# Chosen-token experts: one expert of two batches per unit, with the gated rows as weights

## The reference

```python
k = min(max(int(l * C / e), 1), l)                    # l = 748, C = 2, e = 8: k = 187
S = softmax(x @ Wg); G, I = top_k(swapaxes(S, 1, 2), k)   # each expert of each batch chooses 187 steps
ex = take_along_axis(x[:, None], I[..., None], axis=2)
hmid = gelu(einsum('bekh,ehf->bekf', ex, W1) + b1)    # 128 -> 256
out = einsum('bekf,efh->bekh', hmid, W2) + b2         # 256 -> 128
new_x = zeros.at[batch, I].add(G[..., None] * out)    # h = h + new_x
```

## Time and profile before

| what | us |
| --- | --- |
| median of 3 runs | 2656.92 |
| span of the profiled execution | 2655.1 |
| TensorE busy | 2389.5 (90%) |
| VectorE busy | 2026.5 (76%) |
| ScalarE busy | 1665.8 (63%) |
| GpSimd busy | 1124.6 (42%) |
| `chosen_ffn`, first turned tile to last statistics | 1267.9 to 1640.3 |

### The profile page before, as it was taken

One profiled execution on the slowest core, in us unless ns is written; L12 is line 12 of the kernel. 1 busy time (PEld: TensorE's weight loads), 2 busy tenths in 40 slices (PEclk: granted clock), 3 DMA queues, 4 the chain that ended last, 5 costly groups with the idle time before them and its releaser, 6 DMA issues. The chain is left out here.

```text
span 2655.1 us, 52098 instructions
## 1 busy us (share of the span) xinstructions
PE 2389.5 (90%) x16443; PEld 1819.7 (69%) x16443; DVE 2026.5 (76%) x3647; ACT 1665.8 (63%) x3127; POOL 1124.6 (42%) x1338
## 2 busy tenths in 40 slices
PE   7989699999999999854899997999849999999993
PEld 7989455444445444343799997888738887888882
DVE  4555589999999999489688887788776666787775
ACT  3345267777777777743566664555527777777772
POOL 0016002223223222323777773444337774666664
PEclk9999699999999999975899998999969999999997
DMA  3108633333333323054111112400021113777749
GB/s 90 36 12 319 193 56 50 62 62 56 48 62 62 57 47 62 18 152 149 42 38 38 39 38 68 164 0 0 1 81 52 51 52 103 243 240 247 243 143 277
DMA packets 161298, 249.19 MB, mean 94 GB/s; under 512 B 41645, under 2 KB 106902, under 8 KB 154233
## 3 DMA queue, kind: packets, MB, share of 16 engines
q1 hardware_dynamic: 128888, 208.77, 29.1%
q0 software_dynamic: 19712, 38.13, 4.9%
q10 hardware_dynamic: 12544, 0.39, 0.2%
HBM read 155.24 MB, written 93.41 MB: 94 GB/s over the span
## 5 line engine op out<-in xcount | busy, mean ns | idle before, releaser
L1014 ACT ACTIVATE probs<-score 128x748 f32<-128x748 f32 (+1 forms) x768 | 568.4, 794 | 117.2 <-PE score L839 115.8
L943 DVE TENSOR_REDUCE part_max<-to_dve 128x1 f32<-128x512 f32 (+1 forms) x768 | 479.7, 683 | 84.0 <-PE to_dve L820 83.6
L2762 DVE TENSOR_TENSOR m_hid_lo<-m_up,m_hid_hi 128x512 fp32r<-128x512 f32 x408 | 279.9, 687 | 157.1 <-ACT m_hid_hi L2735 157.1
L820 PE MATMUL to_dve<-k_stack,q_stack 48*128 48x512 f32 (+3 forms) x1536 | 351.4, 367 | 20.9 <-DMA k_stack<-k_parts 20.1
L839 PE MATMUL score<-q_stack,k_stack 49*128 49x374 f32 (+1 forms) x1536 | 317.3, 389 | 3.1 <-ACT probs L1014 1.0
L839 PEld LDWEIGHTS score<-q_stack,k_stack 49*128 49x128 f32 (+1 forms) x1536 | 162.0, 181 | 225.0 <-ACT probs L1014 199.7
L876 PE MATMUL o_sum<-probs,v_sb 128*17 128x374 f32 (+1 forms) x3072 | 315.6, 483 | 0.1
L2658 POOL DMA_INDIRECT e_sums<-m_gated,m_row_in x216 | 212.6, 984 | 162.3 <-DVE m_gated L2780 109.2
L820 PEld LDWEIGHTS to_dve<-k_stack,q_stack 48*128 48x128 f32 (+1 forms) x1536 | 223.1, 187 | 79.7 <-DVE part_max L943 36.6
L740 POOL TENSOR_TENSOR o_rows<-o_raw,inverse 128x384 f32<-128x384 f32 x32 | 26.9, 842 | 589.7 <-DVE inverse L953 589.7
L1371 POOL DMA_INDIRECT f_row_in_c<-c_rows,c_ids x192 | 218.4, 1137 | 75.2 <-issue 49.6
(11 more groups left out here) (411 smaller groups left out, 6003.8 us busy)
## 6 DMA issues: line engine op xcount, KB each, us to landing
m_weights<-e_records SPq DMA_DIRECT2D x54, 1028.0 KB, 6.9
q_stack<-q_parts SPq DMA_DIRECT2D x192, 93.5 KB, 3.1
k_stack<-k_parts SPq DMA_DIRECT2D x192, 93.5 KB, 4.2
e_slots<-blank SPq DMA_DIRECT2D x54, 260.0 KB, 3.9
m_row_in<-e_slots SPq DMA_DIRECT2D x54, 260.0 KB, 3.3
m_weights<-e_sums SPq DMA_DIRECT2D x16, 640.0 KB
e_records<-l_parts SPq DMA_DIRECT2D x16, 512.0 KB, 3.7
v_rows<-v_out SPq DMA_DIRECT2D x16, 408.0 KB, 5.9
```

The lines of the kernel that those rows point to most:

```text
L820: last = pe.matmul(ring[i % RING][0:ROWS[c], at_col:at_col + keys.stop - keys.start], q_stack[its_slot][rows, j, c * P:c * P + ROWS[c]], k ...
L943: dve.tensor_reduce(part_max[0:ROWS[c], k, j, c, 0:1], ring[i % RING][0:ROWS[c], :], AX.X, ALU.max).then_inc(used, 1)
L1014: act.activation(probs[0:n, s % 2, m, 2 * j:2 * j + 2, :], score[tile][0:n, :, 0:HALF], ACT.Exp).then_inc(tile_used, 1)
L2762: dve.tensor_tensor(hid_lo[:, f % RING, :], up[f % UPS][:, :], hid_hi[:, f % RING, :].bitcast(F32), ALU.subtract).then_inc(lo_done, 1)
```

## The change

A unit becomes **one expert of two batches**: partitions 0 to 63 hold slots of the even batch, partitions 64 to 127 those of the odd one. There are again 64 units (8 pairs of batches x 8 experts).

- `widen` and `narrow` have one expert per unit: 6 + 6 matmuls of 384 columns instead of 12 + 12 of 192. There is one bank `up` for both hidden blocks, so the second block waits for the Gelu of the first. Gelu and `keep` are one instruction for 384 columns.
- The gate is column P + e of the gathered record, read in place. `pick_gate` and the owner tiles are gone; the ring has 8 slots and is released by `weigh`.
- In `combine` the gated rows of 64 partitions are the weights (64 x 128, hi and lo apart) and the marks move. The even batch uses the upper row half and the banks of `sums[0]`, the odd one the lower half and `sums[1]`. The band of tile j is cut at step 374: pieces of 374, 252, 310, 316, 246 and 374 steps, for hi and lo, for two halves: 24 matmuls. For the first expert, the first band covers all 748 steps.
- The sums have the features on partitions. Once per two batches ScalarE and VectorE each copy one batch's sums out (`take`), TensorE transposes 12 tiles in 3 groups (`spread`, through the bank `turn`), VectorE adds each group to `h` and takes 12 tiles' statistics, spread over 6 iterations (`returning`).
- The orders are written anew. TensorE in iteration k: widen(k, 0), turn_rows(k+1), narrow(k-1), widen(k, 1), spread, combine(k-2), turn_back(k-1). In `choose` the bases and keys have the new layout.

```diff
-    RING = 5
+    RING = 8
+    GROUP = 4
+    GROUPS_C = 2 * TILES // GROUP
@@ gpsimd
-                    if n >= RING:
-                        pool.wait_ge(turned, n - RING + 1)
+                    if n >= RING:
+                        pool.wait_ge(weighed_n, n - RING + 1)
-                def pick_gate(n):
...
@@ tensor
+                def widen(n, k):
+                    e = expert_of(n)
+                    if k == 0:
+                        pe.wait_ge(split, n + 1)
+                    if n or k:
+                        pe.wait_ge(gelu_done, C_BLOCKS * n + k)
+                    for i, (a, x) in enumerate([(w1_hi, x_hi), (w1_hi, x_lo), (w1_lo, x_hi)]):
+                        last = pe.matmul(up[:, 0:COLS], a[:, e * C_BLOCKS + k, :], x[:, n % 2, :], start=(i == 0), stop=(i == 2))
...
+                def combine(n):
+                    m, e = divmod(n, E_N)
                     pe.wait_ge(gated_n, n + 1)
                     pe.wait_ge(marked, UNIT_TILES * (n + 1))
+                    if e == 0 and m:
+                        pe.wait_ge(act_took, m)
+                        pe.wait_ge(dve_took, m)
+                    for j in range(UNIT_TILES):
+                        for half, cols in pieces(n, j):
+                            for part in range(2):
+                                for o, rows_at in enumerate([slice(0, H), slice(H, P)]):
+                                    last = pe.matmul(sums[o][:, half, cols.start - half * HALF:cols.stop - half * HALF],
+                                                     gated[rows_at, n % 2, j, part, :], marks[rows_at, n % 2, j, cols],
...
                 for k in range(-1, UNITS_C + 2):
                     if valid(k):
-                        widen(k)
+                        widen(k, 0)
+                    if valid(k + 1):
+                        if returning(k) and 1 <= returning(k)[1] <= GROUPS_C:
+                            pe.wait_ge(added, returning(k)[0] * GROUPS_C + returning(k)[1])
+                        turn_rows(k + 1)
                     if valid(k - 1):
                         narrow(k - 1)
-                    if valid(k + 1):
-                        turn_rows(k + 1)
+                    if valid(k):
+                        widen(k, 1)
+                    if returning(k) and returning(k)[1] < GROUPS_C:
+                        m, group = returning(k)
+                        if valid(k + 1):
+                            pe.wait_ge(split, k + 2)
+                        spread(m, group, turn)
                     if valid(k - 2):
-                        combine(k - 2, range(TILES))
+                        combine(k - 2)
                     if valid(k - 1):
                         turn_back(k - 1)
+                for group, bank in enumerate([turn, up, down]):
+                    spread(PAIRS_B - 1, group, bank)
@@ scalar
                 for k in range(-1, UNITS_C + 2):
+                    if returning(k) and returning(k)[1] == 0:
+                        take(returning(k)[0])
                     if valid(k - 2):
                         round_gated(k - 2)
                     if valid(k):
-                        open_hid(k)
+                        open_hid(k, 0)
+                    if valid(k + 1):
+                        round_x(k + 1)
+                    if valid(k):
                         round_hid(k, 0)
                     if valid(k - 1):
                         keep(k - 1)
                     if valid(k):
+                        open_hid(k, 1)
                         round_hid(k, 1)
...
@@ vector
                     if valid(k - 2):
                         weigh(k - 2)
-                    if done is not None:
-                        give_back(done // PER_BATCH)
+                    if returning(k) and returning(k)[1] == 0:
+                        take(returning(k)[0])
                     elif valid(k - 1):
                         mark(k - 1, 0)
                     if valid(k - 2):
                         split_gated(k - 2)
-                    if done is not None and valid(k - 1):
+                    if returning(k) and returning(k)[1] == 0 and valid(k - 1):
                         mark(k - 1, 0)
                     if valid(k - 1):
                         mark(k - 1, 1)
-                    if valid(k):
-                        split_hid(k, 0)
-                    if valid(k - 1):
-                        mark(k - 1, 2)
                     if valid(k + 1):
                         split_x(k + 1)
                     if valid(k):
+                        split_hid(k, 0)
+                    if returning(k) and returning(k)[1] < GROUPS_C:
+                        give_back(*returning(k), turn)
+                    elif returning(k):
+                        measure(returning(k)[0], returning(k)[1] - GROUPS_C)
+                    if valid(k - 1):
+                        mark(k - 1, 2)
+                    if valid(k):
                         split_hid(k, 1)
```

More of the change, by code:

```diff
@@ L1341, in chosen_ffn, with expert_of, band, pieces @@
-        blank_set = sem("f_blank_set")
+                             "f_act_took", "f_dve_took", "f_spread_out", "f_added", "f_padded"))
         gathered = [sem(f"f_gathered{k}") for k in range(RING)]
-        def experts_of(n):
-            return [2 * (n % PER_BATCH) + e for e in range(2)]
-        PICK_BEHIND = 3
+        def expert_of(n):
+            return n % E_N
+        def band(n, j):
+            return slice(0, T) if n % E_N == 0 and j == 0 else BANDS[j]
+        def pieces(n, j):
+            cut = [(h, slice(max(band(n, j).start, half.start), min(band(n, j).stop, half.stop))) for h, half in enumerate(HALVES)]
+            return [(h, cols) for h, cols in cut if cols.start < cols.stop]
@@ L1365, in _ @@
             def _(pool):
[L1366 removed]
+                for n in range(UNITS_C):
                     if n >= RING:
[L1368 removed]
+                        pool.wait_ge(weighed_n, n - RING + 1)
                     for j in range(UNIT_TILES):
@@ L1402, in turn_rows @@
                     last.then_inc(turned, 1)
-                def widen(n):
-                    pe.wait_ge(split, n + 1)
-                    for k in range(C_BLOCKS):
-                        if n:
-                            pe.wait_ge(gelu_done, 2 * C_BLOCKS * (n - 1) + 2 * k + 2)
-                        for m, e in enumerate(experts_of(n)):
-                            cols = slice(m * SLOTS_E, (m + 1) * SLOTS_E)
-                            for i, (a, x) in enumerate([(w1_hi, x_hi), (w1_hi, x_lo), (w1_lo, x_hi)]):
-                                last = pe.matmul(up[k][:, cols], a[:, e * C_BLOCKS + k, :], x[:, n % 2, cols],
-                                                 start=(i == 0), stop=(i == 2))
-                        last.then_inc(up_done, 1)
@@ L1416, in narrow @@
-                def narrow(n):
-                    if n:
-                        pe.wait_ge(kept, 2 * n)
-                    pe.wait_ge(lo_done, C_BLOCKS * (n + 1))
-                    for m, e in enumerate(experts_of(n)):
-                        cols = slice(m * SLOTS_E, (m + 1) * SLOTS_E)
-                        for k in range(C_BLOCKS):
-                            for i, (a, x) in enumerate([(w2_hi, hid_hi), (w2_hi, hid_lo), (w2_lo, hid_hi)]):
-                                last = pe.matmul(down[:, cols], a[:, e * C_BLOCKS + k, :], x[:, n % 2, k, cols],
-                                                 start=(k == 0 and i == 0), stop=(k == C_BLOCKS - 1 and i == 2))
+                def widen(n, k):
[6 more added lines that the diff above has]
+                        last = pe.matmul(up[:, 0:COLS], a[:, e * C_BLOCKS + k, :], x[:, n % 2, :], start=(i == 0), stop=(i == 2))
+                    last.then_inc(up_done, 1)
@@ new lines, in narrow @@
+                def narrow(n):
+                    e = expert_of(n)
+                    if n:
+                        pe.wait_ge(kept, n)
+                    for k in range(C_BLOCKS):
+                        pe.wait_ge(lo_done, C_BLOCKS * n + k + 1)
+                        for i, (a, x) in enumerate([(w2_hi, hid_hi), (w2_hi, hid_lo), (w2_lo, hid_hi)]):
+                            last = pe.matmul(down[:, 0:COLS], a[:, e * C_BLOCKS + k, :], x[:, n % 2, k, :],
+                                             start=(k == 0 and i == 0), stop=(k == C_BLOCKS - 1 and i == 2))
@@ new lines, in spread @@
+                def spread(m, group, bank):
+                    if group == 0:
+                        pe.wait_ge(act_took, m + 1)
+                        pe.wait_ge(dve_took, m + 1)
+                        pe.wait_ge(padded, 1)
+                    for i in range(GROUP):
+                        o, c = divmod(group * GROUP + i, TILES)
+                        last = pe.transpose(bank[:, i * P:(i + 1) * P], summed[:, o, c * P:(c + 1) * P], g.ident[:, :])
+                    last.then_inc(spread_out, 1)
@@ L1569, in _, with take, give_back @@
```

(26 more changed lines are left out.)

157 lines of the change are left out of this document (55 added, 102 removed).

## The result

| what | before | after |
| --- | --- | --- |
| median, us (4 runs each, side by side) | 2655.45 (2653.16 to 2658.15) | 2634.98 (2631.60 to 2637.02) |
| ratio | 1 | 0.9918, 95% interval 0.9904 to 0.9932 |
| span of the profiled execution | 2655.1 | 2635.3 |
| first to last start of `combine` | 1285.50 to 1634.77: 349.3 | 1283.39 to 1614.23: 330.8 |
| last statistics of the stage end | 1640.32 | 1622.20 |

What follows compares the result with a forecast made beforehand. TensorE's order was taken as the bound. Units -21.1, batch ends -23.4, returns +23.9, drain +2.6 and first gather -0.5 sum to -18.5 us, so 2656.9 becomes 2638.4 us, range 2622 to 2662.

Steps and rivals of the forecast that it cites:

- Price of a matmul: In widen and narrow, 12 matmuls of 384 columns at 0.174 us replace 24 of 192: -0.59 us per unit.
- Price of the new combine: In combine, a pair on both row halves costs what one matmul costs: -0.18 us, against +0.4 for mode changes, per unit.
- rivals 1 and 2: In combine: halves run serially, +110 us, chance 0.07; weight loads wait for their half's matmul, +84 us, chance 0.03.
- The change of mode: Around combine, switching between all rows and half rows costs 0.2 us, twice per unit: +0.4 us.
- The ordinary unit: One unit on TensorE takes about 4.88 us instead of 5.21; over 64 units -21.1 us.
- the five terms in brackets: TensorE's work in an ordinary unit: 2.09 + 0.33 + 1.72 + 0.4 + 0.33 us, given as about 4.88.
- Rival 3: The loop through the one bank up becomes the bound: 0.05 to 0.2 us more per unit, 2642 to 2652 us, chance 0.15.
- Between batches: Batch ends removed, 15 x 1.55 = -23.4 us; returns of sums added, 7 times 3.4 = +23.9 us.
- Ends: Start and end of the stage: +2.6 us after the last combine, about -0.5 at the first gather.
- The drain: After the last combine, VectorE needs 6.0 us instead of 3.4: +2.6 us.
- The fill: At the stage's start, the first gather no longer waits for the owner's memsets: about -0.5 us.
- TensorE's order is the bound: In the stage before the change, TensorE runs without a gap in a unit; VectorE's chain shows only between batches.

Runs made afterwards that it cites:

- the wide kernel before: The kernel before with widen and narrow matmuls of 384 columns (first expert's weights for both) and round_x and split_x moved up: 2627.17 us, 0.9892 of before.
- The halves in turn: The changed kernel with all 12 even-half matmuls of combine first, then the 12 of the odd half: 2720.01 us, 1.0241 of before.

## Why the prediction was right, step by step

The forecast was 3.4 us above the median measured. Up to the start of the next stage the trace has lost 18.5 us, the sum's figure to the tenth, and that closeness is luck: the terms below are off by 0.2 to 1.6 us each, with both signs.

- **Price of a matmul.** Right: 0.174 us for 384 columns. The experiment with two of 192 lost 0.5 us per unit where the step said 0.59, and the kernel before with 384 columns and its loop open gained 0.53.
- **Price of the new combine.** Right in mechanism, off in one size: a pair costs what one matmul costs, and weight loads on the same halves cost nothing extra (rivals 1 and 2 fall). Pairs of 374 columns start 0.17 apart, each with new weights. The change of mode is 0.17 on average and not 0.2 us: 0.19 in, 0.14 out. Its sign was misplaced: the first matmul of `combine` and of `turn_back` was to start 0.35 to 0.38 after the one before, and starts 0.27 and 0.255 after it, as the rest of the loss falls in the interval behind it. -0.18 + 0.4 = +0.22 was forecast for the new `combine`; 4.885 - 4.68 = +0.2 is what the two layouts differ by in ordinary units, TensorE being without a gap in both.
- **The ordinary unit.** Right: 4.885 for 4.88, with some luck. The step's two sums don't agree (5.21 - 0.59 - 0.18 + 0.4 is 4.84, the five terms in brackets make 4.87), and small errors cancel: 0.06 less for the mode changes; the first matmul of 384 columns behind three transposes holds TensorE 0.26 us and not 0.174 (1442.83 to 1443.09), twice per unit, and the transposes take 0.25 for the 0.33 of the sum. Rival 3 doesn't decide: over the whole stage TensorE idles 1.6 us for the Gelu, all of it in the fill, although that takes 0.583 us instead of the 0.56 of the estimate, as the groups of the kernel after show:

```profile
L1482 ACT ACTIVATE f_hid_c<-f_up_c,c_b 128x384 f32<-128x384 f32 x128 | 74.6, 583 | 2.1 <-PE f_up_c L1397 2.0
L1397 PE MATMUL f_up_c<-f_x_hi_c,c_w_hi 128*128 128x384 f32 x128 | 52.2, 408 | 2.8 <-ACT f_hid_c L1482 1.6 <-DVE f_x_lo_c L1531 1.2
```

- **Between batches.** Right: 6.49 + 5.79 + 5.78 less three ordinary units is 3.4 us, the sum's figure; the first return costs 0.4 more. Of the 18.4 us between first and last `combine`, 61 ordinary intervals give 20.2 (the sum took 64 units, 21.1; the last two iterations, where TensorE's order is partly empty, gain only 0.1), the batches' ends 22.6 (for 23.4), and the returns take 24.4 (for 23.9).
- **Ends.** The drain is right, +2.4 for +2.6. The fill is mis-sized: -2.1 and not -0.5, and for another reason. The first gather came no earlier. `round_x` and `split_x` moved up take 2.6 us out of the fill of the kernel before, where TensorE idles 1.97 us for `f_x_lo` at 1275.54. In the changed kernel's fill TensorE waits three times for the Gelu instead (0.76, 0.41 and 0.39 us), which may give some of it back; that wasn't tested.
- **"TensorE's order is the bound"** was true of both kernels and yet not the whole answer for the change. The step took 0.59 us per unit from the longer matmuls as if nothing else came next, and walked the new order only. In the old order of ScalarE and VectorE, the same edit met a loop of 5.15 us. The forecast came out right because the change brings the freed loop with it; in pieces the time doesn't add up (the longer matmuls alone gain 5.8 us, the early places alone 8.7, and the changed kernel loses 75 without them).
- **What is still open.** Why the later stages of the same code are 1.3 us shorter in this profile (2.5 in that of the wide kernel before) isn't settled; single executions of one kernel differ by several us, and the kernel before has the longest later stages of all kernels profiled here. The halves in turn were timed in two runs only.

## What to carry to other kernels

Price TensorE's work by start intervals read from rows, and walk every loop that passes through the engine, in the old order as in the new one: a loop just under the bound leaves no wait in an ordinary unit's rows and takes the gain of the first edit that shortens the bound. Test the parts of a change alone and together, since here 5.8 and 8.7 us apart made 29 together. A step that has to wait for another engine belongs behind the work that doesn't need it: moving `spread` behind `combine` gained 13.5 us more.

## What the runs showed of the hardware

- Matmuls on different row halves needn't start in program order: with one half's twelve behind the other's, the odd half's first matmul started about 0.4 us before the even half's last one, in every unit.
- A change from all rows to half rows and back costs 0.34 us together, at a clock of 1.00 (0.345 per unit both with two changes more and with none), and it is spread over two start intervals each way.
- The gathers of GpSimd, 128 rows each, take 1.14 us on average beside its small operations, and 0.99 to 1.03 without them.
